# Attention and feed-forward block on one core: value products one slot later with a fourth turned buffer, queries fetched four slots sooner, masks ahead of the scores, and another order near the end of the feed-forward stage

## The reference

```
x = x + cross_attention(layernorm(x), ctx, lengths, Wq, Wk, Wv, Wo, q_norm, k_norm)  # 16 heads of 64, RMS-normed q and k, key mask
x = x + self_attention(layernorm(x), w_qkv, b_qkv, w_out, b_out)                     # 16 heads of 64, causal
x = x + ffn(layernorm(x), w_gate, w_up, w_down)     # 512 -> 1536 -> 512, 4-bit weights by blocks of 32, 16-bit activations
```

## Time and profile before

| what | value |
|---|---|
| median of 3 runs | 1182.61 us (1180.34 to 1183.07) |
| the profiled execution | 1180.47 us, of which the span of its instructions is 1178.7 us |
| PE matmul busy | 1135.0 us, 96% of the span |
| PE weight loads | 867.6 us, 74% |
| DVE, ACT, POOL busy | 836.7, 738.6, 854.2 us |
| mean granted TensorE clock | 0.996 |
| data moved by DMA | 210.36 MB, 178 GB/s |

### The profile page before, as it was taken

How to read it: one execution, slowest core, us unless ns; L and a number is a source line. 1 busy time by engine, 2 the same in 40 slices (tenths; PEclk the granted TensorE clock), 3 DMA queues, 4 the chain that set the end, 5 groups by cost and what they waited for, 6 DMA issues and landing times. The chain is left out here.

```text
span 1178.7 us, 29367 instructions
## 1 busy us (share of the span) xinstructions
PE 1135.0 (96%) x10784; PEld 867.6 (74%) x10784; DVE 836.7 (71%) x1948; ACT 738.6 (63%) x1335; POOL 854.2 (72%) x745
## 2 busy tenths in 40 slices
PE   7999999999999999999999999999999999899978
PEld 5777778877788788788888888788887678554433
DVE  7778777798767678777667787666676645653685
ACT  6366666776666668667667776666766537612761
POOL 3599899888889888788889878889897732420600
PEclk9999999999999999999999999999999999999989
DMA  8679989999999999999999998999999934795000
GB/s 233 154 137 199 213 177 199 205 225 213 196 204 195 197 196 226 228 192 198 210 190 199 210 236 175 195 205 186 207 186 198 260 86 85 151 230 107 1 1 36
DMA packets 560573, 210.36 MB, mean 178 GB/s; under 512 B 506800, under 2 KB 525232, under 8 KB 560432
## 3 DMA queue, kind: packets, MB, share of 16 engines
q1 hardware_dynamic: 538544, 168.64, 77.6%
q10 hardware_dynamic: 21888, 39.86, 11.9%
HBM read 66.79 MB, written 23.07 MB: 76 GB/s over the span
## 5 line engine op out<-in xcount | busy, mean ns | idle before, releaser
L153 PE MATMUL pair<-arena 128*128 128x256 f16 x2048 | 560.1, 274 | 10.2 <-DVE arena L681 7.7
L155 PE MATMUL pair<-arena 128*128 128x256 f16 x2048 | 559.0, 273 | 0.0
L154 PE MATMUL pair<-arena 128*128 128x256 f16 x2048 | 558.9, 273 | 0.0
L523 POOL TENSOR_TENSOR p_parts<-probs,p_parts 128x512 f16<-128x512 f32 x256 | 313.0, 1227 | 33.8 <-ACT p_parts L630 32.9
L734 DVE CUSTOM_DVE_ANT_0 probs<-bank,mask 128x512 f32<-128x512 f32 x256 | 174.9, 684 | 143.4 <-PE bank L895 133.9
L533 POOL TENSOR_TENSOR k_rinv<-k_ms,half_neg 128x8 f32<-128x8 f32 x128 | 211.3, 1651 | 85.7 <-DVE k_ms L749 85.3
L153 PEld LDWEIGHTS pair<-arena 128*128 128x128 f16 x2048 | 200.1, 98 | 84.3 <-issue 51.3
L630 ACT ACTIVATE p_parts<-probs 128x512 f16<-128x512 f32 x256 | 161.0, 629 | 143.9 <-DMA pt<-p_parts 134.7
L155 PEld LDWEIGHTS pair<-arena 128*128 128x128 f16 x2048 | 200.6, 98 | 23.6
L154 PEld LDWEIGHTS pair<-arena 128*128 128x128 f16 x2048 | 200.6, 98 | 20.8
L607 ACT ACTIVATE probs<-probs,neg_max 128x512 f32<-128x512 f32 x256 | 183.0, 715 | 8.8 <-DVE neg_max L743 8.7
(11 more groups left out here) (310 smaller groups left out, 1719.2 us busy)
## 6 DMA issues: line engine op xcount, KB each, us to landing
raws<-in_ctx_t_dram SPq DMA_DIRECT2D x58, 256.0 KB, 3.9
side_kept<-side_parts ACTq DMA_DIRECT2D x40, 256.0 KB, 4.6
arena<-side_kept SPq DMA_DIRECT2D x40, 256.0 KB, 4.5
w_kept<-ffn_turned ACTq DMA_DIRECT2D x36, 256.0 KB, 3.1
side_raw<-in_w_qkv_dram ACTq DMA_DIRECT2D x24, 256.0 KB, 3.5
arena<-w_kept SPq DMA_DIRECT2D x24, 256.0 KB, 4.5
pt<-p_parts SPq DMA_TRANSPOSE x240, 4.3
ffn_raw<-in_w_gate_dram ACTq DMA_DIRECT2D x12, 256.0 KB, 4.0
```

Of the source, the lines that this page charges most:

```text
L153: nc.tensor.matmul(to, x_hi[k], w_hi[k], start=(k == 0), stop=False)
L154: nc.tensor.matmul(to, x_hi[k], w_lo[k], start=False, stop=False)
L155: mm = nc.tensor.matmul(to, x_lo[k], w_hi[k], start=False, stop=(k == n - 1))
L523: nc.gpsimd.tensor_tensor(p_parts[n % PTS][:, 1, :], probs[n % PROBS][:, :], p_parts[n % PTS][:, 0, :], ALU.subtract).then_inc(p_lo_done, 1)
```

## The change

Cross attention:

- Value products of parts 0 to 243 come 19 slots behind the projections, the last 12 come 18 behind; slot 262 does two of them.
- `p_parts` and `pt` have 4 buffers; `v_both` has 10.
- The sums at the end of a unit come one slot later on DVE, ACT, POOL and SP, in odd slots instead of even ones. In DVE's order they now stand after k_ms and v_lo.
- Each of the 16 masks is written at the end of the slot ahead of the one that reads it.
- Queries are fetched in slot 8u + 1 instead of 8u + 5, except for unit 4.

Feed-forward:

- ACT no longer rounds gate tile 0 (POOL does it after its last `sig_i`) and no longer copies up tile 11 (DVE does it after it has handed the maximum to PE). ACT takes gate tiles 1 to 9 and then waits for the scale of UP.
- DVE takes the maximum over up tiles 0 to 10 beforehand and joins it with that of tile 11 in the operation that scales it.
- `signed` of tile 1 moves from ahead of the first split to behind it; from there on DVE's loop is: split k, signed k + 1, signs k + 2.
- PE's filler is 3 matmuls more when raw_done 3 comes, 2 instead of 3 after each of the products 6 to 10, and 4 and then 3 instead of 5 and then 1 after the last spread.

```diff
-CTX_RAWS, KTS, VS, PROBS, PTS, QS = 4, 3, 11, 10, 3, 3
+PV_LATER = PARTS - 12
+CTX_RAWS, KTS, VS, PROBS, PTS, QS = 4, 3, 10, 10, 4, 3
-Q_LOAD = 5
+Q_LOAD, Q_LOAD_KEPT = 5, 1
+MASKS_AT = SCORE_LAG
+        def value_slot(n):
+            return n + PV_LAG + (n < PV_LATER)
+        def values_at(slot):
+            return [n for n in (slot - PV_LAG - 1, slot - PV_LAG) if 0 <= n < PARTS and value_slot(n) == slot]
...
+        def q_unit_loaded(slot):
+            u, at = divmod(slot - Q_LOAD_KEPT, 8)
+            if at == 0 and 0 < u < B * GROUPS and u != GROUPS // 2:
+                return u
+            return GROUPS // 2 if slot == 8 * (GROUPS // 2) + Q_LOAD else None
...
-                if (n := part(PV_LAG, slot)) is not None:
+                for n in values_at(slot):
...
+            pool.wait_ge(raw_done, 2)
+            nc.gpsimd.tensor_scalar(gate_i[:, 0, :], gate_raw[:, 0, :], raw_inv[:, ACTED:ACTED + 1], None, ALU.mult).then_inc(gi_pool_done, 1)
...
             busy(bank[1], WARM_PRODUCT)
+            pe.wait_ge(raw_done, 3)
+            busy(bank[1], WARM_PRODUCT)
             for k in range(KF - 1):
                 pe.wait_ge(prod_done, k + 1)
-                busy(bank[1], WARM_PRODUCT)
+                busy(bank[1], WARM_PRODUCT if k < KF // 2 else 2)
             top_spread(PRODUCT)
-            busy(bank[1], 5)
-            pe.wait_ge(oi_done, 1)
-            busy(bank[1], 1)
+            busy(bank[1], 4)
+            pe.wait_ge(raw_done, 4)
+            busy(bank[1], 3)
...
-            for k in range(EARLY[0]):
-                acted_int(k)
+            acted_int(1)
             kept(2 * KF - 2)
-            for k in range(EARLY[0], EARLY[1]):
-                acted_int(k)
-            act.wait_ge(last_top_done, 1)
-            nc.scalar.activation(up_raw[:, KF - 1, :], ring[(2 * KF - 1) % 4][:, :], ACT.Copy, scale=1.0 / W_UP).then_inc(last_kept, 1)
-            for k in range(EARLY[1], READY):
+            for k in range(2, KF - len(LATER)):
                 acted_int(k)
...
-            nc.vector.tensor_scalar(tops[:, 1, KF - 1:KF], last_top[:, :], 1.0 / W_UP, None, ALU.mult).then_inc(tops_done, 1)
-            dve.wait_ge(tops_done, 2 * KF)
-            nc.vector.tensor_reduce(mine[:, UP:UP + 1], tops[:, 1, :], AX_X, ALU.max).then_inc(mine_done, 1)
+            nc.vector.tensor_scalar(mine[:, UP:UP + 1], last_top[:, :], 1.0 / W_UP, up_top[:, 0:1], ALU.mult, ALU.max).then_inc(mine_done, 1)
+            nc.vector.tensor_scalar(up_raw[:, KF - 1, :], last_up, 1.0 / W_UP, None, ALU.mult).then_inc(last_kept, 1)
...
             signs(BARE_TILES[0])
-            signed(BARE_TILES[0])
```

More of the change, by code:

```diff
@@ L325, in x_batch, with masked_chunk @@
             return X_AT.index(slot - lag) if slot - lag in X_AT else None
+        def masked_chunk(slot):
+            b, at = divmod(slot - MASKS_AT, 2 * CHUNKS * GROUPS)
+            return (b, at // 2) if 0 <= b < B and at % 2 == 0 and at < 2 * CHUNKS else None
         def pair_of_scores(slot):
@@ L345, in cross_attention @@
         LAST = PARTS + PV_LAG
+        def value_slot(n):
+            return n + PV_LAG + (n < PV_LATER)
+        def values_at(slot):
+            return [n for n in (slot - PV_LAG - 1, slot - PV_LAG) if 0 <= n < PARTS and value_slot(n) == slot]
         def whole_unit(lag, slot):
-            n = part(PV_LAG + lag, slot)
-            return n // 8 if n is not None and n % 8 == 7 and n < PARTS - 1 else None
+            ends = [n for n in values_at(slot - lag) if n % 8 == 7 and n < PARTS - 1]
+            return ends[0] // 8 if ends else None
         def batch_at(lag, slot):
@@ L443, in _ @@
                     sp.dma_start(g["q_kept"][Q_UNITS[m][0], Q_UNITS[m][1]], q_turned).then_inc(q_out, 16)
-                u, at = divmod(slot - Q_LOAD, 8)
-                if at == 0 and 0 < u < B * GROUPS:
+                u = q_unit_loaded(slot)
+                if u is not None:
                     wait(sp, s_done, CHUNKS * (u - QS + 1))
@@ L705, in _ @@
                 d = slot // 2 - 1
-                if (n := part(PV_LAG + 1, slot)) is not None and n % 8 == 7 and n < PARTS - 1:
-                    u = n // 8
-                    dve.wait_ge(pv_done, n + 1)
+                if (u := whole_unit(1, slot)) is not None:
+                    dve.wait_ge(pv_done, 8 * u + 8)
                     wait(dve, o_done, u - 1)
@@ L721, in _ @@
                     if u % GROUPS == 0 and h == 0:
[L723 to L727, removed]
                         dve.wait_ge(mask_done, CHUNKS * b + k + 1)
@@ L771, in _ @@
                     left_of_batches()
+                if (at := masked_chunk(slot)) is not None:
+                    b, k = at
+                    if at == (0, 0):
+                        dve.wait_ge(ready, 1 + 2 * VS)
+                    wait(dve, s_max_done, 8 * (GROUPS * b - 1) + 2 * k + 2)
+                    nc.vector.tensor_scalar(mask[:, k, :], key_no[:, :], left[:, b, k:k + 1], NEG, ALU.is_ge,
+                                            ALU.mult).then_inc(mask_done, 1)
                 if (b := x_batch(0, slot)) is not None and b:
@@ L1547, in feed_forward @@
     GATE, ACTED, UP, PRODUCT = range(4)
-    EARLY, READY = (1, 5), 10
+    LATER = {5: 10, 7: 11}
     BARE_TILES = tuple(range(1, KF))
@@ L1805, in _ @@
                 dve.wait_ge(up_act, k + 1)
-                dve.wait_ge(gi_done, k + 1)
+                if k:
+                    dve.wait_ge(gi_done, k)
+                else:
+                    dve.wait_ge(gi_pool_done, 1)
                 if k in BARE:
@@ L1820, in _ @@
             signs(BARE_TILES[0])
-            signed(BARE_TILES[0])
             nc.vector.tensor_scalar(y_scale[:, :], scale[:, PRODUCT:PRODUCT + 1], 1.0 / W_UP, None, ALU.mult).then_inc(ysc_done, 1)
             for k in range(KF):
-                if k in BARE and BARE[k] + 1 < len(BARE):
-                    signs(BARE_TILES[BARE[k] + 1])
-                    signed(BARE_TILES[BARE[k] + 1])
                 dve.wait_ge(oi_done, k + 1)
@@ L1831, in _ @@
                 nc.vector.tensor_tensor(o_lo[k % 3][:, :], up_i[:, k, :], o_hi[k % 3][:, :], ALU.subtract).then_inc(ol_done, 1)
+                if k + 1 in BARE:
+                    signed(k + 1)
+                if k + 2 in BARE:
+                    signs(k + 2)
             dve.wait_ge(ysc_done, 1)
```

25 lines of the change are left out of this document (15 added, 10 removed).

## The result

The changed kernel takes 1171.81 us (median of 4 runs, 1170.95 to 1172.08); the kernel before took 1182.19 in the same session. The ratio is 0.9914 (95% interval 0.9899 to 0.9929). The forecast was 1170.0, in a range of 1166.5 to 1177. The number was right. The parts of the sum behind it were not all right, and that is what the experiments are about.

What follows compares the result with a forecast made beforehand. PE was taken as the bound, so cross attention could win only its waits. Powers 7.5, queries 2.4, masks 0.4, feed-forward 2.2, less 1.0, make 11.5 us: 1169.0 profiled, 1170.0 with half the spread; range 1166.5 to 1177.

Steps and rivals of the forecast that it cites:

- Powers, 7.5 less 1.0: Cross attention: a deadline one slot later removes eight PE waits for turned powers, 7.5 us, less 1.0 at unit ends.
- The second half of the argument: Cross attention: ACT needs an earlier part's landing, so its 3.42 us idle shrinks and the turns start sooner; within the 7.5.
- The cost of 1.0 at the unit ends: 31 unit ends: DVE's sum waits for PE's value product, so PE may wait; 0 to 3 us, 1.0 taken.
- Queries, 2.4: Cross attention: queries fetched four slots sooner remove all five "issue" waits ahead of the scores, 2.4 us, at most 3.4.
- the sum of 11.5: Whole kernel: powers 7.5, queries 2.4, masks 0.4, feed-forward 2.2, less 1.0, taken off the profiled 1180.47 us.
- The first rival: Cross attention: SP's queue is the bound and the wait moves, only a third of 7.5 won: 1175 us, chance 0.18.
- "nothing": Cross attention: lateness stays tied to the deadline, so the change wins only 2.2 us: 1180.4, chance 0.07.
- the stall at every unit's end: 31 unit ends: PE's first value product waits for the sum, 0.7 each, 21.7 us in all: about 1192, chance 0.04.
- Masks, 0.4: Cross attention: one PE wait of 0.9 us for a read of the scores possibly goes; 0 to 0.9, 0.4 taken.
- Feed-forward, 2.2: Feed-forward: first up_i starts 1.5 us sooner, less PE filler gives 0.2, the first split ahead of signed 0.5.
- that rival: Down projection: thinner filler brings a 6.8 us stretch at half clock, costing 3.4: 1173.5 us, chance 0.09.
- The spread: Whole kernel: median is 2.1 us above the profiled execution, probably late landings; half is added, giving 1170.0.

Runs made afterwards that it cites:

- e4: Kernel before with four buffers of p_parts and pt and ten of values, value products still 18 slots behind: 1181.21 us, ratio 0.9989.
- e3: Kernel before with only the feed-forward's new order, cross attention as before: 1179.67 us, ratio 0.9975.
- g2: The changed kernel measured once more, nothing altered: 1168.11 us, ratio 0.9880 to the kernel before.
- g4: Changed kernel with the masks written again with the scores of each batch's first unit: 1170.79 us, ratio 0.9905 to the kernel before.
- e1: Kernel before with value products 19 slots behind, four buffers of p_parts and pt, ten of values: 1185.94 us, ratio 1.0034.
- e2: Kernel before with queries fetched at slot 8u+1 and masks written at their own slots: 1175.15 us, ratio 0.9941.
- f5: Kernel before with only the queries fetched at slot 8u+1: 1177.60 us, ratio 0.9955.
- f6: Changed kernel with the queries fetched at slot 8u+5 again: 1180.84 us, ratio 0.9981 to the kernel before.
- f8: Changed kernel with the block of output products issued ahead of the slot's scores: 1167.92 us, ratio 0.9867 to the kernel before.
- g3: f8 plus DVE's copy of the last up tile moved behind the scale of up: 1169.02 us, ratio 0.9883 to the kernel before.
- g1: Changed kernel with three buffers of split and turned powers instead of four, still 19 slots behind: 1197.94 us, ratio 1.0122 to the kernel before.

## Why the prediction was right, and which step was not

**Powers, 7.5 less 1.0.** The mechanism was right: a deadline one slot later takes in the lateness. The landing of a turned power came 3.0 us ahead of its product before (median of 240) and 6.2 in the changed kernel, under 1 us in 36 of 240 and then in 5, and the row went from 5.9 to at most 0.5 in the traces at lag 19 and four buffers. The second half of the argument, that ACT's shorter idle brings the turns forward, is not borne out: e4 has the shorter idle and no fewer waits. The size was too large even beside early queries: 5.0 by the stream where 6.5 were forecast, and the lists of waits account for about 3 of the 5. Alone it is nothing by the stream (868.0 against 867.9) and a loss by the times (ratio 1.0034).

The cost of 1.0 at the unit ends was not seen: o_sum stays at 0.7 once for PE, and in the stream of the traces at lag 19 with four buffers PE waits for no read of the scores. In the tail, where DVE has the sum of a unit just ahead of a read, that wait (ahead of pair 126) was 0.1 in the first trace before and is 1.4 in the first after; but it is 0.7 in e3, which has the old order, and 0.7 in g2, which has the new one, so the change need not be its cause. DVE did stand ahead of the sum, 15.6 us in 17 of the 31 units (41.9 in 22 before), but that cover was enough. In a unit where it had a weight tile to do first it went on without a wait:

```profile
609.29 0.43 DVE L731 TENSOR_REDUCE o_sum<-bank 128x130 f32<-128x260 f32 x1
...
610.43 0.68 DVE L749 CUSTOM_DVE_ANT_0 probs<-bank,mask 128x512 f32<-128x512 f32 x1
```

**Queries, 2.4: the step that failed.** "All five waits go, 2.4": they went, and the term was mis-sized. It is 6.0 by the stream (5.3 by the times) in the kernel before, and 9.7 by the medians in the changed one (1180.84 against 1171.1; 11.1 by the stream). I priced each wait as if it stood for itself, and took the lead of 2.74 at unit 8 for the rule, where it was the shortest of 30. The waits for powers and queries together were 8.3, 7.3 and 9.1 in the three traces with both deadlines tight, 8.0 and 12.3 with the powers' deadline relaxed, 2.9, 1.6 and 3.7 with the queries' relaxed, at most 0.5 with both and the fourth buffer. So they behave as two deadlines for one lateness, that of SP's turns and loads, and PE pays at whichever is left. Early queries take the row for powers down with them, from 5.9, 4.9 and 7.4 to 2.9, 1.6 and 3.7, and this with their own row is 5.5 of the 6.0. Why the turns land in better time when the load moves isn't shown; that it left the slots where SP is behind would fit.

That the sum of 11.5 still came close is in part luck. The queries were priced 3.6 us too low, the powers 1.5 too high, and the tail, which no term had, is 1.3 longer on average in the three traces of the changed order (after, g2, g4) than in the three with late queries and lag 18. Stream, feed-forward and tail together give 11.0 + 2.5 - 1.3 = 12.2, and the medians 11.2 (1182.3 less 1171.1). The size also needed all parts together. For the parts alone the same sum failed: e1 was 10 us above it, e2 4 below, f5 2.4 below, and f6, the whole without the queries, 6.6 above.

**The first rival** (the queue is the bound, the wait moves) was told of the whole change and got 0.18. It is what the lag does alone. Its argument against, that a stretch without waits exists, says nothing of bursts. The rule I cited with it, from the Trainium skill (Perfetto Trace Analysis, What "DMA-bound" means), speaks of an issuing engine whose track is solid with DMA slices. In the window ahead of the largest stall of f6 (492.00 to 498.20) SP's issues fill 5.7 of the 6.2 us, so in the bursts the trace leans to it; between 550 and 690 us of the kernel before, where PE waits for nothing, they fill 118 of 140. Of the other two that were priced for cross attention, "nothing" falls with a stream that is 11 us shorter, and the stall at every unit's end with the 0.7 once.

**Masks, 0.4.** The size is within what the runs can tell, the reason was wrong. The wait of 0.9 for a read of the scores (at 245.24 before) is there in all six traces at lag 18, in e2 with moved masks and in e4 with ACT relieved too, and in none of the seven at lag 19 with four buffers. It went with the lag.

**Feed-forward, 2.2.** 2.5 by the stages. In the first trace, against the stage's own start (1060.30 before, 1053.68 after, 6.62 sooner): the first `up_i` 1.16 where 1.5 was forecast, because DVE's copy of the last up tile came ahead of the scale, which is 0.44 later; from there to the rounded product another 0.41, of which less filler is 0.32 (forecast 0.2): PE loads the maximum 0.05 after it is written instead of 0.37; the split 0.51 behind that (0.5). Half of the stretch at the low clock went too in this trace (3.4 us instead of 6.8). The window of 7 us from the scale of up on, to be held against the earlier trace rows:

```profile
1120.70:1127.70 7.00, 6.59 (x25) 2.14 (x24) 6.33 (x21) 6.11 (x10) 0.00 (x0) 0.84 0.00 0
```

PE is busy for 6.59 us where it was 3.49, and the clock 0.84 where it was 0.51. No fall follows in the down projection (0.38 us for the product at 1134.08), so that rival didn't come where I looked for it. It came in the tail instead: the wait of 2.24, of which the prediction said only that it stays, was followed by half clock in the first trace, and with the longer wait at pair 126 it makes its tail 2.3 us longer.

**The spread.** I took half of the 2.1 us between the profiled execution and the median for late landings that the change absorbs. The kernel before ran from 1178.5 to 1190.6 over all sessions, the changed one from 1167.6 to 1172.1 in 8 runs: that fits, but it doesn't show it, as the 8 are few beside some seventy and g4, all but the same kernel, has one at 1177.2. The lower end of the range, 1166.5, left out the half of the spread that the upper end has in it.

## What to carry to other kernels

Where several waits on one engine hang from the same late queue, they don't add: relax one deadline and the next one collects, so move all deadlines of that queue together, and test a part by taking it out of the whole, not only by adding it alone. A later deadline needs its buffer (26 us for the missing one here), and a buffer without the later deadline was worth nothing that the times show. Before believing a gain of 0.3%, run the base again in the same session.

## What the runs showed of the hardware

The same standstill of PE, 2.24 us ahead of the scores of pair 125, is in 12 of the 14 traces (all but f8 and g3). In seven of them the granted clock went to half within 1.5 us of its end and stayed there for 3.4 us, in five it did not, and the changed kernel has one trace of each kind. With the fall the tail is 2.2 us longer at lag 19 (40.1 to 40.2 against 38.0) and 0.7 to 1.1 at lag 18. With the stalls of 2.7 and 3.2 us in f6 it fell both times, and once behind one of 1.1 (e4, 275.54), while e1's stalls of 1.9 and 1.8 had none: in this range the length of a stall alone doesn't tell.

The time from issue to landing of a turned power was the same in the kernels that differed by 14 us: 4.3 us (median of 240) in the kernel before, 4.2 in the changed one, 4.3 in e1 and f6, and 4.0 in g1, the slowest. What changed the time was how late a landing was allowed to be.
